# A memory-and-expert layer in a four-layer model: how its pipeline is filled, and what stands in the middle of a step

## The reference

```python
x = x + L1_attn(layernorm(x))
x = x + L1_ffn(layernorm(x))

def L1_attn(x):                                   # x: (8, 512, 128)
    Bm, Cm = x @ W_B + b_B, x @ W_C + b_C
    dt = softplus((x @ W_dt1 + b_dt1) @ W_dt2 + b_dt2)
    phi = cumsum(omega_base * dt, axis=1)
    content = Bm * x
    real = cumsum(content * cos(phi), axis=1)
    imag = cumsum(content * sin(phi), axis=1)
    return (Cm * (real * cos(phi) + imag * sin(phi))) @ W_out + b_out + D * x

def L1_ffn(x):                                    # 16 experts of width 64, one shared of width 128
    scores = softmax(x @ gate_w.T)
    # keep the 2 best of 4 groups of experts, then the 4 best experts in them
    y = sum over the chosen experts e of scores[e] * (silu(x @ w1[e]) * (x @ w3[e])) @ w2[e]
    return y + (silu(x @ ws1) * (x @ ws3)) @ ws2
```

## Time and profile before

| | us |
|---|---|
| median of three runs | 1530.38 |
| the profiled execution | 1523.88 |
| its span (first to last instruction) | 1522.1 |
| the block of this layer, from its first POOL instruction to the last `down` | 664.5 to 1027.3 |
| filling (before the first `up`) | 664.5 to 766.3 |
| step 0 / step 1 / steps 2 to 7 | 42.1 / 33.8 / 185.1 |

### The profile page before, as it was taken

The page is one execution under the profiler, slowest core; times in us unless marked ns, Lnnn a source line. Parts: engine busy times, 40 slices in busy tenths (PEclk is TensorE's granted clock), DMA queues, the critical chain, the costliest instruction groups (busy, mean ns, idle before and its releaser), DMA issues. The chain is left out here.

```text
span 1522.1 us, 22941 instructions
## 1 busy us (share of the span) xinstructions
PE 1306.6 (86%) x7286; PEld 774.0 (51%) x7286; DVE 1021.8 (67%) x2781; ACT 788.3 (52%) x1579; POOL 534.1 (35%) x678
## 2 busy tenths in 40 slices
PE   4899999999997878944479999988899998999898
PEld 1223333333322768932346565567666766877633
DVE  7778888888863675635887776324566663666576
ACT  1467777767774104526556553312555453466554
POOL 3443442344110006348555335431122122433056
PEclk7899999999998888975689999999999999999999
DMA  5211111111103502210052323221131221000001
GB/s 152 62 45 31 54 53 43 43 54 35 48 16 107 129 1 65 60 37 24 11 109 61 56 57 57 70 43 41 61 118 60 84 92 61 30 2 1 1 22 35
DMA packets 80779, 81.23 MB, mean 53 GB/s; under 512 B 19899, under 2 KB 64139, under 8 KB 80659
## 3 DMA queue, kind: packets, MB, share of 16 engines
q1 hardware_dynamic: 77327, 74.06, 18.5%
q0 software_dynamic: 2304, 4.72, 1.4%
q10 hardware_dynamic: 1028, 0.98, 0.2%
HBM read 64.32 MB, written 13.92 MB: 51 GB/s over the span
## 5 line engine op out<-in xcount | busy, mean ns | idle before, releaser
L955 DVE TENSOR_REDUCE a_nm<-a_aps 128x1 f32<-128x512 f32 x512 | 330.0, 686 | 72.8 <-PE a_aps L709 72.8
L919 ACT ACTIVATE a_prob<-a_sps 128x512 f32<-128x512 f32 x512 | 270.1, 599 | 114.5 <-PE a_sps L722 114.1
L709 PE MATMUL a_aps<-a_K,a_Q 96*128 96x512 bf16 x512 | 189.8, 396 | 27.5 <-DMA a_K<-k_parts 26.1
L722 PE MATMUL a_sps<-a_Q,a_K 99*128 99x512 bf16 x512 | 155.9, 384 | 1.3 <-ACT a_prob L919 1.3
L1421 POOL TENSOR_TENSOR p_h<-p_sl,p_t 128x512 f32<-128x512 f32 x72 | 106.4, 1494 | 140.9 <-ACT p_sl L1564 86.4
L732 PE MATMUL a_ops<-a_prob,a_Vg 128*32 128x512 f32 x1024 | 136.8, 608 | 0.0
L709 PEld LDWEIGHTS a_aps<-a_K,a_Q 96*128 96x128 bf16 x512 | 50.3, 98 | 151.9 <-DVE a_nm L955 89.5
L1564 ACT ACTIVATE p_sl<-p_up_a 128x512 f32<-128x512 f32 x72 | 42.9, 597 | 109.1 <-PE p_up_b L1449 109.1
L1959 POOL TENSOR_TENSOR c_h<-c_h,c_G 128x512 f32<-128x512 f32 x24 | 32.1, 1341 | 171.0 <-DMA c_G<-choice_rows 131.1
L413 POOL CAST a_ms<-a_mr 16x128 bf16<-16x128 f32 x32 | 9.0, 280 | 232.2 <-ACT a_mr L876 232.2
L722 PEld LDWEIGHTS a_sps<-a_Q,a_K 99*128 99x128 bf16 x512 | 49.6, 98 | 67.9 <-ACT a_prob L919 37.6
(11 more groups left out here) (582 smaller groups left out, 2767.9 us busy)
## 6 DMA issues: line engine op xcount, KB each, us to landing
p_G<-gates_by_expert SPq DMA_DIRECT2D x32, 512.0 KB, 10.1
c_G<-choice_rows SPq DMA_DIRECT2D x32, 512.0 KB, 6.3
a_Q<-q_parts SPq DMA_DIRECT2D x192, 32.0 KB
a_K<-k_parts SPq DMA_DIRECT2D x31, 96.0 KB
q_parts<-a_partsq SPq DMA_DIRECT2D x7, 384.0 KB, 2.8
k_parts<-a_partsk SPq DMA_DIRECT2D x7, 384.0 KB, 2.8
token_outputs<-m0e_y SPq DMA_DIRECT2D x40, 64.0 KB, 1.5
m0w_w<-in_L_ffn_W SPq DMA_DIRECT2D x1, 2048.0 KB, 8.5
```

The lines of the kernel that those rows point to most:

```text
L709: nc.tensor.matmul(aps[n % 3][:, :], Q[0:MAX, head, q * P:(q + 1) * P], K[0:MAX, head, :], start=True, stop=True).then_inc(a_ready, 1)
L722: nc.tensor.matmul(sps[(NS * u + k) % 3][:, :], K[0:KB, head, q * P:(q + 1) * P], Q[0:KB, head, :], start=True, stop=True).then_inc(s_read ...
L919: nc.scalar.activation(prob[u % 2][:, j, q, :], sps[n % 3][:, :], ACT.Exp).then_inc(p_done, 1)
L955: nc.vector.tensor_reduce(nm[u % 2][:, s:s + 1], aps[n % 3][:, :], AX.X, ALU.max, negate=True).then_inc(a_used, 1)
```

## The change

The loop of 17 steps becomes a filling written out instruction by instruction and eight steps. Chunk 0 is taken alone as far as it goes: its gather is the first instruction on POOL, and its normalising is on DVE. `choose` and `shift_logits` of chunk 1 come in the middle of step 0, as do the memory of chunks 1 and 2; the filling ends before they are done. The lookahead gets shorter by one chunk at each stage: step s now does `outer` of s + 2, `input_gates` and content of s + 3, first transposes and softplus of s + 4, `measure_first` and `first_root` of s + 5. So the memory of chunk 3 and the phase of chunk 4 fall into step 1.

Work changes engine: `add_back` from chunk 2 on goes from DVE to POOL; the copy of the shared unit from DVE to ACT (`keep_shared`); `first_normal` of chunks 0 and 1 from POOL to DVE, of 4 to 7 to ACT; the sine products of chunks 1 and 2 to POOL (`turn_content`, `turn_memory`). `down` runs unit by unit and waits for each `h` alone, and between its units stand `turn_second` and `logits`. For chunk 0, PE spreads the gates of the first four pairs itself (`choose_pair`: a product with a matrix of zeros and ones, `of_pair`, made by two `affine_select` on POOL; `keep_pair` copies it into `G`), and SyncE spreads the other four. `trig` stands in the middle of the units, under the table that silu uses.

```diff
--- before.py
+++ after.py
...
+            fetch_back(0)
             nc.gpsimd.memset(one[:, :], 1.0)
             nc.gpsimd.memset(half_pi[:, :], math.pi / 2).then_inc(consts, 1)
+            fetch_back(1)
...
+            fetch_back(2)
+            fetch_back(3)
+            add_back(2)
+            add_back(3)
+            add_bias(0)
+            add_bias(1)
+            nc.gpsimd.memset(of_pair[:, :, :], 1.0).then_inc(pair_ones, 1)
...
+            fetch_back(4)
+            first_normal(2)
+            first_normal(3)
+            add_back(4)
+            add_bias(2)
+            fetch_back(5)
+            add_bias(3)
+            turn_content(1)
+            turn_memory(1)
...
+            def down(c, j):
+                if j == 0:
                     wait(pe, y_added, c)
-                for j in range(NW):
+                pe.wait_ge(h_done, NW * c + j + 1)
+                for k in range(TC):
...
+            def choose_pair(j):
+                if j == 0:
+                    pe.wait_ge(gT_done, 1)
+                    pe.wait_ge(pairs_made, 1)
+                wait(pe, G0_done, j)
+                nc.tensor.matmul(whole_yps, of_pair[:, j, :], gT[0][:, :], start=True, stop=True).then_inc(chosen, 1)
...
+            def middle(s):
+                pe.wait_ge(a_done, NW * (s + 1))
+                if here(s + 2):
+                    outer(s + 2)
+                if here(s + 3):
+                    input_gates(s + 3)
+                if here(s + 4):
+                    turn_first(s + 4)
+                pe.wait_ge(t_done, NP * (s + 1))
+                if here(s + 4):
+                    steps_of_time(s + 4)
+                for j in range(NW):
+                    down(s, j)
+                    if j == 1 and here(s + 2):
+                        turn_second(s + 2, up_a[1])
+                    if j == 3 and here(s + 2):
+                        logits(s + 2, up_b[1])
...
+            turn_first(0)
+            steps_of_time(0)
+            input_gates(0)
+            turn_first(1)
+            steps_of_time(1)
+            outer(0)
+            turn_first(2)
+            steps_of_time(2)
+            input_gates(1)
+            turn_second(0, up_a[1])
+            logits(0, up_b[1])
+            turn_first(3)
+            steps_of_time(3)
+            up(0, 0)
+            up(0, 1)
+            turn_gates(0, whole_yps)
+            choose_pair(0)
+            for j in range(2, NW):
+                if j <= BY_PE:
+                    choose_pair(j - 1)
+                up(0, j)
+                if j == 3:
+                    outer(1)
+                    input_gates(2)
+                if j == 5:
+                    turn_second(1, ops)
+                if j == 6:
+                    logits(1, ops)
+            turn_gates(1, ops)
...
+            def keep_shared(c):
+                act.wait_ge(up_done, NW * c + 1)
+                wait(act, h_done, NW * c - 2)
+                nc.scalar.activation(t[NW * c % 3][:, :], up_b[NW * c % 2][:, :], ACT.Copy).then_inc(shared_kept, 1)
...
+            def middle(s):
+                if here(s + 2):
+                    nc.scalar.preload_act_table(ACT.Sqrt)
+                if here(s + 4):
+                    copy_first(s + 4)
+                if here(s + 2):
+                    second_root(s + 2)
+                if here(s + 5):
+                    first_root(s + 5)
+                if here(s + 2):
+                    second_normal(s + 2)
+                if here(s + 4):
+                    softplus_parts(s + 4)
+                if here(s + 2):
+                    copy_second(s + 2, up_a[1])
+                if here(s + 4):
+                    softplus_exp(s + 4)
+                if here(s + 2):
+                    gate_exponentials(s + 2)
+                if here(s + 4):
+                    softplus_log(s + 4)
+                if here(s + 2):
+                    nc.scalar.preload_act_table(ACT.Silu)
...
+            first_root(0)
+            copy_first(0)
+            softplus_parts(0)
+            first_root(1)
+            softplus_exp(0)
+            softplus_log(0)
+            copy_first(1)
+            softplus_parts(1)
+            softplus_exp(1)
+            softplus_log(1)
+            nc.scalar.preload_act_table(ACT.Silu)
+            trig(0)
+            nc.scalar.preload_act_table(ACT.Sqrt)
+            first_root(2)
+            first_root(3)
+            copy_first(2)
+            second_root(0)
+            nc.scalar.preload_act_table(ACT.Exp)
+            softplus_parts(2)
+            copy_second(0, up_a[1])
+            gate_exponentials(0)
+            copy_first(3)
+            softplus_exp(2)
+            softplus_parts(3)
+            softplus_exp(3)
+            softplus_log(2)
+            softplus_log(3)
+            nc.scalar.preload_act_table(ACT.Silu)
+            trig(1)
+            silu(0, 0)
...
+                    silu(s, j)
+                    if j == 0:
+                        keep_shared(s)
+                    if s == 1 and j == 0:
+                        trig(3)
+                    if here(s + 3) and j == 4:
+                        trig(s + 3)
+                    if here(s + 1) and j == MID:
+                        keep_gates(s + 1, ops)
+                    if here(s + 4) and j == 6:
+                        first_normal(s + 4)
...
+            def middle(s):
+                if here(s + 5):
+                    measure_first(s + 5)
+                if here(s + 2):
+                    add_memory(s + 2)
+                    second_rstd(s + 2)
+                if here(s + 5):
+                    first_rstd(s + 5)
+                if here(s - 1):
+                    measure_output(s - 1)
+                if s == 0:
+                    phase_sum(3)
+                    phase_rest(3)
+                elif here(s + 3):
+                    take_content(s + 3)
+                    turn_content(s + 3)
+                    sum_cosines(s + 3)
+                if here(s + 2):
+                    shift_logits(s + 2, up_b[1])
+                    choose_groups(s + 2)
+                    choose_experts(s + 2)
...
+            phase_sum(0)
+            phase_rest(0)
+            measure_first(2)
+            v.drain()
+            measure_first(3)
+            take_content(0)
+            turn_content(0)
+            sum_cosines(0)
+            sum_sines(0)
+            first_rstd(2)
+            first_rstd(3)
+            turn_back(0)
+            read_memory(0)
+            phase_sum(1)
+            add_memory(0)
+            second_rstd(0)
+            second_normal(0)
+            phase_rest(1)
+            shift_logits(0, up_b[1])
+            choose_groups(0)
+            choose_experts(0)
+            take_content(1)
+            turn_content(1)
+            sum_cosines(1)
+            sum_sines(1)
+            product(0, 1)
+            turn_back(1)
+            product(0, 2)
+            read_memory(1)
+            phase_sum(2)
+            product(0, 3)
+            add_memory(1)
+            measure_first(4)
+            second_rstd(1)
+            first_rstd(4)
+            phase_rest(2)
+            product(0, 4)
+            product(0, 5)
+            take_content(2)
+            turn_content(2)
+            sum_cosines(2)
+            product(0, 6)
+            shift_logits(1, ops)
+            sum_sines(2)
+            choose_groups(1)
+            choose_experts(1)
+            product(0, 7)
+            turn_back(2)
+            product(0, 8)
+            read_memory(2)
+            middle(0)
...
+                    if s == 1 and j == 1:
+                        take_content(3)
+                        turn_content(3)
+                    if s > 1 and here(s + 3) and j == 1:
+                        phase_sum(s + 3)
+                    product(s, j)
+                    if s == 1 and j == 1:
+                        sum_cosines(3)
+                    if s == 1 and j == 2:
+                        phase_sum(4)
+                        phase_rest(4)
+                    if s > 1 and here(s + 3) and j == 2:
+                        phase_rest(s + 3)
+                    if here(s + 2):
+                        if j == 4:
+                            sum_sines(s + 2)
+                        if j == 5:
+                            turn_back(s + 2)
+                        if j == 6:
+                            read_memory(s + 2)
```

409 lines of the change are left out of this document (221 added, 188 removed).

## The result

| | before | after | predicted |
|---|---|---|---|
| median, us | 1530.38 | 1515.06 | 1495 (1478 to 1514) |
| ratio, 95% interval | | 0.9912 [0.9892, 0.9933] | 0.977 |
| first `up`, from the block's start T | T+101.8 | T+57.0 | T+59.4 |
| step 0 | 42.1 | 67.4 | 59.1 |
| step 1 | 33.8 | 41.1 | 37 |

What follows compares the result with a forecast made beforehand. Bounds: a chain of latencies in the filling, PE in steps 2 to 7. Gain 25.4 to step 1's start, loss 3.2 in step 1, gain 13.1 in steps 2 to 7: 35.3, so 1495 us (1478 to 1514).

Steps and rivals of the forecast that it cites:

- The filling to the first `up`: Filling: chunk 0 taken alone shortens the latency chain, first `up` at T+59.4 where it was at T+101.8.
- the holes at the end of the units: Steps 2 to 7: six PE holes of 2.4 us shrink to 0.7, giving 9 to 10 of the 13.1 gain.
- 28.7 in a step, under PE's 31.9: Steps 2 to 7: DVE's work per step, 28.7 us, stays below PE's 31.9, so DVE does not bound.
- the clock's rise: Steps 2 to 7: without the holes PE's clock rises from 0.95, counted as 4 us of gain.
- 21.8 with its wait: Step 1, units: DVE owes 21.8 us including 3 of waiting for ACT, where PE's units take 15.5.
- the 4 for contention: Step 0: 4 us added for DVE and POOL getting in each other's way.
- 5.5 of waits: Step 0: DVE's named waits: two POOL sine products of 1.4, ACT's turn 2, logits behind `down` 0.7.
- 24.5 and a middle of 15: Step 0: PE's 15.5 of pairs and some 9 of others, plus its middle, fit beside DVE's list.
- the 85% that I gave as the sign: Step 0: sign that the forecast holds, DVE busy over 85% and PE waiting for it.
- A: Rival, chance 0.20: filling gives back more in step 0 because PE runs at low clock; gain 12 to 25, about 1512.
- the late tile: Filling: if `affine_select` is slow, POOL's normalised tile of chunk 2 comes 11 late, costing up to 10 us.
- C: Rival, chance 0.05: contention with POOL makes DVE the bound, costing 47 us; time 1542; decisive when a step passes 39.

Runs made afterwards that it cites:

- b2: Kernel before with only the middle rearranged: `down` unit by unit, second transposes and logits between its units, eight steps of lookahead kept; ratio 0.9918 to before.
- a3: Changed kernel with DVE's long memory operations one to a unit and two edits at PE's waits for the last silu and second transposes; ratio 0.9826 to before.
- a5: Changed kernel without the skip term `xT` x `Dg` in the memory's output for chunks 4 to 7; ratio 0.986 to before.
- the short product: POOL writes 128 of 512 columns of its product, `down` reads only those; ratio to before 0.9817 in the changed kernel, 0.9979 in the one before.
- c1: Changed kernel with only DVE's long memory operations placed one to a unit; ratio 0.9875 to before.
- k1: Changed kernel with the second half of chunk 4's phase behind product 3 of step 1, not product 2; ratio 0.9906 to before.
- j2: j1 with DVE's list of step 1 spread over units 1 to 7; ratio 0.9833 to before.
- a4: Changed kernel with chunk 1's choice of experts behind products 7 and 8 and chunk 2's memory, its gates turned later on PE; ratio 0.988 to before.
- j1: Changed kernel with the edits of a3 and a4 together; ratio 0.9797 to before, the fastest version.
- j3: j2 with eight useless 128x128 matmuls into a free bank behind chunk 0's turned gates; ratio 0.9843 to before.

## Why the prediction was wrong

*Right.* The filling to the first `up` (T+57.0 against T+59.4), with the first transposes at T+10.6 (I had T+10.7) and the first silu at T+63.4 (T+65.8). That the holes at the end of the units go: in the old kernel that part alone gave 11.2 us in steps 2 to 7, where I had 13.1. Against my times step 0 is 8.3 us too long, step 1 4.1 and steps 2 to 7 11.1; less the 2.4 by which the filling is shorter that is the 21.1 that the block lacks of the 35.3.

*Steps 2 to 7, the largest miss: 2.0 gained and not 13.1.* The failing step is "28.7 in a step, under PE's 31.9". The number was right (DVE was busy 28.4, 29.3 and 27.4 us in steps 2 to 4), but I held DVE's whole list against PE's whole step. DVE spends the middle in a chain with waits, and it is the units that must hold the rest: they grew from 16.4 to 17.7 and 18.6 us in steps 2 to 4, with `up` waiting for `p_t`. I also left PE's list as it was. With five steps of lookahead one chunk more of `outer`, input gates, first transposes and step sizes falls into these steps; against b2 PE is busy 6.9 us longer, and the clock's rise, which I did forecast, only paid for it. In steps 4 and 5 the first transposes that had covered the second normalisation are missing: waits of 1.1 and 2.8. Shown: b2 (173.9 without the short lookahead) and a3 (173.1 with it, most of the waits taken away). How much of the 9.2 between after and b2 is work and how much waits is not settled; in a5, meant for that, times and profile disagree.

*Step 1: 41.1 and not 37.* The term was mis-sized: DVE's list in the units was put at 21.8 with its wait, and the units took 25.2. With the short product they take 21.2, near my number, and the step 37.1. So contention, which I counted in step 0 only, was missing here; the 4.0 us hold the clock's rise from 0.92 to 1.00 as well, which the run does not part from it. Other orders of the same list gave 1.1 us at best (a3, c1) and lost in k1 and j2.

*Step 0: 67.4 and not 59.1.* From the first silu to the first `up` of step 1 it took 61.0 us where I had 52.7 (T+65.8 to T+118.5):

```profile
735.69:796.71 61.02, 45.68 (x183) 26.56 (x184) 44.59 (x136) 31.13 (x53) 29.75 (x24) 0.80 0.23 62
```

DVE was busy 44.6 of them, where my list with the 4 for contention has 47.2 up to that point, so the list was not too short. It stood idle 16.4, and I had named 5.5 of waits: that term failed. The choice of experts for chunk 1 stood ahead of products 7 and 8 and of `r`; PE waited 6.74 for its gates and 2.73 for `r`, and DVE then for PE's `outer`. Moving it gave 4.9 (a4). PE's work did not fit in as I had it either: it was busy 51.7 us of step 0, for which I had 24.5 and a middle of 15, at a clock of 0.79; from 741 to 750 and behind the wait at 778.86 its rows are those of the low level. What the low level cost there no run isolates. The 4 for contention came out about right: the short product gives 3.9. DVE was busy 67% of the step, not the 85% that I gave as the sign.

*The rivals.* A named the time best (1512), with half of its reason: the clock in step 0 was 0.79 where it had been 0.92, though not at the low level throughout, and the late tile did not come (each `affine_select` took 1.1 us). C was right in mechanism and wrong in size: the short product is worth 15 us, not 47, and only step 1 passes its 39.

## What to carry to other kernels

When a change lengthens an engine's list inside a loop, compare it with the bounding engine in each part of the step, not over the whole step: a total with 10% to spare can hide a stretch that is over. A shorter lookahead moves work from a stretch where engines idle into one where they don't; list what moves for every engine. And test the parts alone: one half of this change gave all of its gain, the other paid for its own 15 us within seven steps, until a few small edits in the order made both count (a3, j1).

## What the runs showed of the hardware

When an instruction of DVE with two SBUF inputs and a product of POOL lie beside each other, the one that starts second pays. The same running sum of `p_cs` in step 2 and in step 5 of the changed kernel (POOL's products are drawn together in one row):

```profile
847.87 5.10 POOL L1452 TENSOR_TENSOR p_h<-p_sl,p_t 128x512 f32<-128x512 f32 x3 [2.56 <-DVE p_t L1847]
848.24 1.98 DVE L1869 TENSOR_TENSOR_SCAN p_mem<-p_one,p_cs 128x512 f32<-128x512 f32 x1
...
949.57 1.22 DVE L1869 TENSOR_TENSOR_SCAN p_mem<-p_one,p_cs 128x512 f32<-128x512 f32 x1
949.80 3.74 POOL L1452 TENSOR_TENSOR p_h<-p_sl,p_t 128x512 f32<-128x512 f32 x2 [0.45 <-DVE p_t L1847]
```

The eight steps hold 63 such instructions of the memory and the phase. Of these 24 began while POOL's instruction was running, and each lost what was left of it less 0.12 to 0.14 us (0.91 left at 848.24: 1.98 and not 1.22). Another 8 began first and lost nothing, and POOL's product took 1.59 or 2.06 us and not 1.27. The other 31 had none beside them. So it is not the unit that counts: the sum took 1792 ns on average at unit 4 in after, where it began second in three of four steps, and 1217 at unit 3 in a3, where it began first in all. In c1 and a3 the long instructions stand singly behind the products that POOL waits for, and DVE's busy time in steps 2 to 7 fell from 118.9 to 114.3; in j2 the spread went the other way, because three of step 1 began second and lost 0.9 to 1.1 each, where in j1's the largest such loss is 0.4. `TENSOR_SCALAR` with one input is not free of it: the one of L1894 took 0.48 to 0.53 us in seven places and 1.55 at 874.60, beside a product of POOL. The product `p_t`, which reads PSUM, took 0.66 to 0.69 in all 64 places.

In the profiled execution of a5 two steps with less work for PE were longer than in after: the granted clock was 0.90 in a step that had run at 1.00, behind waits of 0.7 and 2.4 us where that step had had 0.7 and 2.8. Step 5 of c1, with no work taken away, ran at 0.95. I can't say from these runs which short wait lets it fall. Nor did eight products into a free bank hold it up (j3).
